# Experts by place: each token only through its two experts, from lines sorted in memory

## The reference

```
x = x + attn_a(layernorm(x))   # per batch a 64x64 rotation polynomial, a codebook row, RMS norm
x = x + experts(layernorm(x))
x = x + attn_b(layernorm(x))   # 16 heads of 8, softmax over 1024 tokens, output projection
x = x + experts(layernorm(x))  # the same weights again

experts(h):  logits = h @ router.T            # 8 experts
             top 2 of the logits, softmax over the two
             y_e = relu(h @ w1[e])**2 @ w2[e] # w1[e] 128x256, w2[e] 256x128
             out = sum over the two chosen e of weight * y_e
```

## Time and profile before

| | |
|---|---|
| median of three runs | 1290.02 us |
| profiled execution, its time | 1291.25 us |
| its span, first to last instruction | 1289.5 us |
| mean granted TensorE clock | 0.960 |
| PE, DVE, ACT, POOL busy | 93%, 76%, 75%, 22% |
| DMA queue of SP | 6014 packets, 9.45 MB, 2.1% of 16 engines |

### The profile page before, as it was taken

The page is one execution under the profiler, slowest core; times in us unless marked ns, Lnnn a source line. Parts: engine busy times, 40 slices in busy tenths (PEclk is TensorE's granted clock), DMA queues, the critical chain, the costliest instruction groups (busy, mean ns, idle before and its releaser), DMA issues.

```text
span 1289.5 us, 25719 instructions
## 1 busy us (share of the span) xinstructions
PE 1197.6 (93%) x10019; PEld 742.1 (58%) x10019; DVE 976.4 (76%) x2357; ACT 960.9 (75%) x1826; POOL 285.5 (22%) x326
## 2 busy tenths in 40 slices
PE   1779999998899999999999999999999999999998
PEld 1369999987434434444444444444444348999998
DVE  7575677766888898989898888988889814565654
ACT  1037777765158998888898888988888996777775
POOL 2032000003423333332332333332322100000000
PEclk9679999999569999999999999999999999999999
DMA  5100000000000000000000000000000000000000
GB/s 193 36 1 1 1 1 1 2 1 1 1 1 1 2 1 2 2 1 2 2 2 1 2 2 1 2 1 2 1 2 1 1 2 1 9 17 9 10 9 17
DMA packets 6134, 11.08 MB, mean 9 GB/s; under 512 B 1907, under 2 KB 3574, under 8 KB 5878
## 3 DMA queue, kind: packets, MB, share of 16 engines
q1 hardware_dynamic: 6014, 9.45, 2.1%
HBM read 7.28 MB, written 2.10 MB: 7 GB/s over the span
## 4 chain that ended last, share of the span: by engine, by line
PE 78%; DVE 13%; ACT 6%; issue 3%; DMA 0%; SPq 0%; ACTq 0%; DVEq 0%
PE acc L1280 17%; PE six L1115 17%; PE six L1251 10%; DVE mxp L947 8%; PE six L1103 6%; PE six L1105 5%; PE six L1104 5%; PE misc L1251 5%; ACT PB L645 3%; PE six L1264 2%; PE six L1217 1%; ACT SC L634 1%; PE six L1127 1%; PE six L1212 1%; PE misc L1103 1%
## 5 line engine op out<-in xcount | busy, mean ns | idle before, releaser
L947 DVE TENSOR_REDUCE mxp<-six 128x2 f32<-128x1024 f32 x512 | 598.8, 1219 | 75.4 <-PE six L1264 73.4
L645 ACT ACTIVATE PB<-six 128x512 f32<-128x512 f32 x681 | 384.9, 599 | 60.7 <-PE six L1251 36.9
L1280 PE MATMUL acc<-PB,Vg 128*32 128x256 f32 x4096 | 328.0, 392 | 16.3 <-ACT SC L634 16.3
L1264 PE MATMUL six<-K,Q 32*128 32x512 f32 x1024 | 264.1, 519 | 14.4 <-DVE mxp L947 9.7
L1251 PE MATMUL six<-Q,K 32*128 32x512 f32 x681 | 272.5, 498 | 0.1
L1115 PEld LDWEIGHTS six<-w2s,PB 128*128 128x128 f32 x2048 | 248.2, 192 | 11.3 <-ACT PB L547 0.7
L1115 PE MATMUL six<-w2s,PB 128*128 128x128 f32 x2048 | 249.3, 275 | 0.1
L850 DVE SCALAR_TENSOR_TENSOR x<-six,wexp,x 128x128 f32<-128x128 f32 x512 | 144.2, 345 | 134.9 <-PE six L1115 134.2
L541 ACT ACTIVATE PB<-six 128x512 f32<-128x512 f32 x256 | 151.2, 599 | 114.8 <-PE six L1105 104.4
L645 ACT ACTIVATE PB<-misc 128x512 f32<-128x512 f32 x343 | 205.4, 599 | 23.2 <-PE six L1251 17.1
L1251 PEld LDWEIGHTS six<-Q,K 32*128 32x128 f32 x681 | 107.9, 183 | 142.7 <-ACT PB L645 73.4
(11 more groups left out here) (225 smaller groups left out, 1094.7 us busy)
## 6 DMA issues: line engine op xcount, KB each, us to landing
x<-in_x SPq DMA_DIRECT2D x4, 512.0 KB, 5.1
SC<-in_w_om SPq DMA_DIRECT2D x1, 2048.0 KB, 14.6
out<-x SPq DMA_DIRECT2D x8, 256.0 KB, 2.0
VH<-in_w SPq DMA_DIRECT2D x1, 1024.0 KB, 9.2
Vg<-in_wqs SPq DMA_DIRECT2D x1, 256.0 KB, 8.0
Vg<-in_wks SPq DMA_DIRECT2D x1, 256.0 KB, 7.4
cst<-in_cst SPq DMA_DIRECT2D x1, 81.5 KB, 3.4
nwb<-in_nw SPq DMA_DIRECT2D x1, 64.0 KB
```

Of the source, the lines that this page charges most:

```text
L645: act.activation(PB[:, s % 3, j, :], scores, ACT.Exp).then_inc(G_("act_taken"), 1)
L947: dve.reduce_max(dst, taken_slot("max", s, i).rearrange("p (a n) -> p a n", a=2), AX.X).then_inc(G_("max_taken"), 1)
L1264: ins = pe.matmul(slot[:, c * BLK:(c + 1) * BLK], Q[rows, G % NG, t * P:(t + 1) * P], K[rows, G % NG, th * BLK:(th + 1) * BLK], start=True ...
L1280: ins = pe.matmul(acc[RB * j:RB * (j + 1), n], Vg[:, G % 2, t, j, :], PB[:, s % 3, j, n], start=(t == 0 and half == 0), stop=(t == TPB - 1 ...
```

## The change

The dense expert layer goes, in both layers. Each batch of 1024 tokens has 2048 (token, expert) pairs. They get a place in a list sorted by expert, in which each expert's part is rounded up to whole tiles of 128 lines; `RT` = 23 tiles hold every case. Per batch, for layer f:

- DVE normalises the batch (`rows`), PE transposes and runs the router in fp32 (`turn_rows`, `batch_router`), DVE takes the top two (`batch_top_two`), PE counts by triangular and all-one matmuls how many pairs stand before each (`batch_rank`, 16 matmuls), DVE works out the place of each pair and the expert of each tile (`batch_places`): `dest`, `te` (for SP) and `tw` (for PE).
- GpSimd sends each of the batch's 8 tiles of tokens twice to its places in a DRAM buffer `xs` (`send`, 16 indirect DMAs of 128 rows of 512 bytes). SP has filled the buffer with zeros at the start (`empty_lines`).
- SP loads the sorted lines in six groups of up to four tiles (`load_lines`), and, for each tile, the w1 of its expert from DRAM by a register (`load_weights`, 23 DMAs of 128 KB, three groups ahead). The registers are read from `te`, up to four at a time. w1 is no longer kept or split.
- PE reads up to four registers from `tw`, transposes the lines (`turn_lines`), makes the hidden values by fp32 matmuls of 128x128 (`lines_hidden`, a pair of tiles at a time), DVE takes relu (`relu_pair`), ACT squares (`square_pair`), PE makes the results two pairs later with w2 addressed by register (`lines_result`), ACT copies out the transposed lines and the results (`lines_out`, `result_out`), SP stores the results to a DRAM buffer `yd` (`keep_lines`).
- GpSimd fetches the two result rows of each token (`fetch`, 16 indirect DMAs), DVE adds them with their weights (`add_results`).

Where things stand: in layer 0 batches 0 and 1 are routed before the loop, 2 and 3 beside batches 0 and 1. Results of batch 0 are fetched and added during batch 3, those of batches 1 to 3 during attention (`late_results`, and GpSimd's fetches in groups -1 to 3), where the statistics for attention now stand too (`late_stats`). `attention_begin` follows the loop. In layer 1 batches 0 to 2 are routed in the last attention group (`routed_late`), batch 3 beside batch 0; `attention_end` runs as one piece before the loop; results of batches 1 to 3 are added after it. `RMS_GROUPS` has four groups. GpSimd builds the triangle `tri` at the start. The diff, cut to its core:

```diff
-RMS_GROUPS = ((0, 2), (2, 2), (4, 4))
+RMS_GROUPS = ((0, 2), (2, 2), (4, 2), (6, 2))
...
+LN_BLOCKS = (NBLK, 0, NBLK)
+SEND = 2 * TPB
+RT = (2 * L + E * (P - 1)) // P
+TG = 4
+RGROUPS = -(-RT // TG)
+PAIRS = -(-RT // 2)
...
+            def send(f, b):
+                n = sparse_index(f, b)
+                pl.wait_ge(G_("dest_ready"), n + 1)
+                if f == 0:
+                    pl.wait_ge(G_(f"emptied{b}"), 16)
+                for i in range(TPB):
+                    for k in range(2):
+                        pl.indirect_dma_start(xs[b], bass.IndirectOffsetOnAxis(ap=dest[:, b, k, i:i + 1], axis=0),
+                                              hbs[:, b, i, :], None).then_inc(G_(f"sent{b}"), 16)
...
+            def fetch(f, b, i):
+                for k in range(2):
+                    pl.indirect_dma_start(lines_back[b][:, k, i, :], None, yd[b],
+                                          bass.IndirectOffsetOnAxis(ap=dest[:, b, k, i:i + 1], axis=0)
+                                          ).then_inc(G_(f"back{b}{i // TPK}"), 16)
...
+            def load_lines(f, b):
+                n = sparse_index(f, b)
+                sp.wait_ge(G_(f"sent{b}"), 16 * SEND * (f + 1))
+                if n >= 2:
+                    sp.wait_ge(G_("lines_turned"), RGROUPS * (n - 1))
+                for g in range(RGROUPS):
+                    if n:
+                        sp.wait_ge(G_(f"line{g}"), 16 * (min(TG, RT - TG * g) + 1) * n)
+                    if f and b == 0 and g == 4:
+                        sp.wait_ge(G_("act_filled"), len(AR))
+                    t = slice(TG * g, min(RT, TG * (g + 1)))
+                    sp.dma_start(lines_in[b][:, t, :], xs[b].rearrange("(r p) d -> p r d", p=P)[:, t, :]
+                                 ).then_inc(G_(f"line{g}"), 16)
...
+            def load_weights(f, b, g):
+                n = RGROUPS * sparse_index(f, b) + g
+                sp.wait_ge(G_("te_ready"), sparse_index(f, b) + 1)
+                if n >= 3:
+                    sp.wait_ge(G_("hidp_done"), pair_count(n - 3))
+                for i, e in enumerate(expert_values(SP, te, b, g, E - 1)):
+                    sp.dma_start(w1t[:, n % 3, i * HID:(i + 1) * HID],
+                                 a["w1"][ds(e, 1)].rearrange("o d h -> (o d) h")).then_inc(G_(f"line{g}"), 16)
...
+                for m in range(RGROUPS * B):
+                    if m % RGROUPS == RGROUPS - 3 and m // RGROUPS + 1 < B:
+                        load_lines(f, m // RGROUPS + 1)
+                    if m + 3 < RGROUPS * B:
+                        load_weights(f, *divmod(m + 3, RGROUPS))
+                    if m:
+                        keep_lines(f, *divmod(m - 1, RGROUPS))
...
-            low_part(3, 0)
-            for n in range(1, NBLK):
-                low_part(3, n)
+            for b in range(3):
+                send(1, b)
+            fetch_batch(1, 0)
+            send(1, 3)
+            for b in range(1, B):
+                fetch_batch(1, b)
...
+            def batch_rank(f, b):
+                pe.wait_ge(G_("both_ready"), sparse_index(f, b) + 1)
+                if f == 0 and b == 0:
+                    pe.wait_ge(G_("tri_ready"), 1)
+                rank, all_lines = route_bank(f, b)[:, 128:128 + TPB * E], route_bank(f, b)[:, 192:192 + E]
+                pe.matmul(rank, tri[:], both[:], start=True, stop=False, skip_group_check=True)
+                for d in range(1, TPB):
+                    pe.matmul(rank[:, d * E:], ones[:], both[:, 0:(TPB - d) * E], start=False, stop=(d == TPB - 1),
+                              skip_group_check=True)
+                for i in range(TPB):
+                    ins = pe.matmul(all_lines, ones[:], both[:, i * E:(i + 1) * E], start=(i == 0), stop=(i == TPB - 1))
+                ins.then_inc(G_("rank_done"), 1)
...
+                link(dve.tensor_scalar(tilesi[:], route_bank(f, b)[:, 192:192 + E], float(P - 1), None, ALU.add))
+                link(dve.tensor_scalar(tilesi[:], tilesi[:], 7, None, ALU.arith_shift_right))
+                link(dve.tensor_copy(tilesf[:], tilesi[:]))
+                link(dve.tensor_tensor(upsum[:], tilesf[:].rearrange("p (o e) -> p o e", o=1).broadcast_to([P, E, E]),
+                                       upto[:], ALU.mult))
+                link(dve.reduce_sum(ends[:], upsum[:], AX.X))
+                link(dve.tensor_tensor(firstr[:], ends[:], tilesf[:], ALU.subtract))
+                link(dve.tensor_scalar(firstr[:], firstr[:], float(P), -1.0, ALU.mult, ALU.add))
+                link(dve.tensor_tensor(place[:], rank, firstr[:].rearrange("p (o e) -> p o e", o=1)
+                                       .broadcast_to([P, TPB, E]), ALU.add))
...
+            def turn_lines(f, b, g):
+                n = RGROUPS * sparse_index(f, b) + g
+                pe.wait_ge(G_("tw_ready"), sparse_index(f, b) + 1)
+                pe.wait_ge(G_(f"line{g}"), line_count(f, b, g))
+                if f and b == 0 and g == 1:
+                    pe.wait_ge(G_("acc_stored"), 8 * B)
+                if n >= 2:
+                    pe.wait_ge(G_("lines_stored"), n - 1)
+                for i, at in enumerate(expert_values(PE, tw, b, g, CH * D * (E - 1))):
+                    r = TG * g + i
+                    expert_at[b, r] = at
+                    ins = pe.transpose(line_bank(n)[:, i * P:(i + 1) * P], lines_in[b][:, r, :], ident)
...
+                        ins = pe.matmul(big[:, n % 2, at:at + P], tile_weights(group, r % TG, c), lines,
+                                        start=True, stop=True)
...
+                        ins = pe.matmul(big[:, 2 + group % 2, r % TG * D:(r % TG + 1) * D], sqs[:, n % 3, at:at + P],
+                                        w2f[:, ds(expert_at[b, r] + c * D, D)],
...
+                turn_lines(f, 0, 0)
+                for s in range(PAIRS * B):
+                    b, q = divmod(s, PAIRS)
+                    if q % 2 == 0 and s + 2 < PAIRS * B:
+                        turn_lines(f, *divmod(s // 2 + 1, RGROUPS))
+                    lines_hidden(f, b, q)
+                    if s >= 2:
+                        lines_result(f, *divmod(s - 2, PAIRS))
+                    route = routed_beside(f, b)
+                    if route and q in (5, 6):
+                        turn_rows(f, route, q - 5)
+                    elif route and q == 7:
+                        batch_router(f, route)
+                    elif route and q == 9:
+                        batch_rank(f, route)
...
+            def add_results(f, b, u):
+                dve.wait_ge(G_(f"back{b}{u}"), 16 * TPB * (f + 1))
+                for k in range(2):
+                    for i in range(TPK * u, TPK * (u + 1)):
+                        xt = x[:, b * L + i * D:b * L + (i + 1) * D]
+                        ins = dve.scalar_tensor_tensor(out=xt, in0=lines_back[b][:, k, i, :],
+                                                       scalar=pw[:, b, k, i:i + 1], in1=xt, op0=ALU.mult, op1=ALU.add)
+                    if k == 0:
+                        link(ins)
+                ins.then_inc(G_("mixed"), 1)
...
+            late_stats = {(0, 1): 2, (0, 9): 3, (2, 9): 4, (3, 9): 5, (4, 9): 6, (5, 9): 7}
+            late_results = {(-1, 14): (1, 0), (-1, 15): (1, 1), (1, 4): (2, 0), (2, 4): (2, 1), (3, 4): (3, 0),
+                            (4, 4): (3, 1)}
```

More of the change, by code:

```diff
@@ L310, in bank_a2, with line_bank, route_bank, rows_bank @@
             return six[:, n, :] if n < 6 else acc[:] if n == 6 else six[:, 3, :]
+        def line_bank(n):
+            return acc[:] if n % 2 else s1[:, 0, :]
+        def route_bank(f, b):
+            return six[:, 0, :] if f == 0 and b == 0 else s1[:, 1, :]
+        def rows_bank(f, b):
+            return six[:, 3, :] if f and b < 3 else misc[:]
+        def pair_count(n):
+            return PAIRS * (n // RGROUPS) + min(PAIRS, 2 * (n % RGROUPS) + 2)
+        def line_count(f, b, g):
+            return 16 * (min(TG, RT - TG * g) + 1) * (sparse_index(f, b) + 1)
+        def wait_kept(engine, f, b):
+            for k in range(3):
+                engine.wait_ge(G_(f"kept{k}"), 16 * RGROUPS // 3 * (sparse_index(f, b) + 1))
+        def tile_weights(n, i, c):
+            return w1t[:, n % 3, i * HID + c * P:i * HID + (c + 1) * P]
+        def first_bank(task):
+            return misc[:] if task % 2 else acc[:]
+        def routed_beside(f, b):
+            return (b + 2 if b < 2 else None) if f == 0 else 3 if b == 0 else None
+        def expert_values(engine, values, b, g, top):
+            _, experts = nc.values_load_multi_w_load_instructions(
+                values[0:1, b, TG * g:min(RT, TG * (g + 1))], engines=[engine], min_val=0, max_val=top,
+                skip_runtime_bounds_check_because="DVE bounds each of them when it writes them")
+            return experts
         @block.sync
@@ L450, in _ @@
             low_part(2, 0)
[L451 removed]
             low_part(2, 1)
[L453 removed]
+            for t in range(4):
```

(24 more changed lines are left out.)

656 lines of the change are left out of this document (413 added, 243 removed).

## The result

The changed kernel takes 1470.98 us (median, 1469.26 to 1472.79), the kernel before 1289.88 in the same comparison: ratio 1.1404, 95% interval 1.1384 to 1.1424, slower. The forecast was 1182 us. Times are medians of all executions of a kernel, ratios leave out the executions in a slower state, so that the two can differ a little (E6, E16).

What follows compares the result with a forecast made beforehand. It took TensorE to bound the expert layers (98% busy), with PE 96%, DVE and ACT 88% busy in attention. 1289.5 - 63 (layer 0) + 12 + 17 - 74 (layer 1) = 1181.5 us of span; predicted 1182, range 1125 to 1275.

Steps and rivals of the forecast that it cites:

- The indirect DMA: GpSimd's sends and fetches: 1.2 us each, bounds 0.46 and 2.03; a batch's 16 sends take 19.2 us.
- batch 3's chain: Layer 1: batch 0's results stored, 16 fetches, 16 sends, load; 74 us, wanted at 77, so hidden.
- TensorE per batch, 26.8 us: Expert layers' batch pace: matmuls 20.5 us, transposes 2.4, register reads 4; 26.8 us against 54.
- First expert matmul at 131.5: Layer 0's start: routing, sends, landing and line load put the first expert matmul at 131.5 us, 38 later.
- fits with nothing to spare; from 1.4 us an issue on, TensorE waits: Layer 0, batch 2's sends: start after destinations (157), land before batch 2 (about 179); 16 x 1.2 + 4.5 us.
- SP costs 16 us a batch: SP's queue in the expert layers: 35 issues at 0.46 us, 16 us a batch, six register reads on top.
- My rival of transfers and SP: Expert layers: transfers or SP set the pace, 36 us a batch, adding 74 us, total 1256; chance 0.20.
- Attention +12: Attention: added DVE results and statistics cost 5.5 us in the prelude and 6.5 elsewhere, 12 us longer.
- The last group +17: Attention's last group: added transposes, router and rank matmuls 19 us, 5.5 hidden, waits 3.5; 17 us longer.
- My rival of a low clock: Expert layers: TensorE falls to half clock, a batch takes 50 us, total 1368; chance 0.04.
- The tail of 29 us: Layer 1's end: copy, store, sixteen fetches, landing, results and last store after TensorE's last matmul, 29.4 us.
- GpSimd as the bound: Indirect DMAs in GpSimd's one queue are the bound; gain gone at about 2.4 us each, 1345 at 3.0; chance 0.12.

Runs made afterwards that it cites:

- E6: E1 with w1 kept in SBUF, each tile taking a fixed expert's, so the 184 weight loads go and results are other ones: 1333.86 us, 1.0310.
- E16: E13 with layer 0's line loads for batches 1 to 3 issued by GpSimd behind its own sends, not by SP: 1321.69 us, 1.0215.
- E4: The kernel before, plus four bursts of 16 back-to-back indirect fetches in the dense layer 1, which nothing waits for: 1350.66 us, 1.0472.
- E1: The changed kernel, with GpSimd waiting after every fourth indirect DMA of a send or whole-batch fetch until those landed: 1361.38 us, ratio 1.054.
- E15: The changed kernel with the changes of E2, E6 and E7, and attention's results and statistics in small parts, all at once: 1193.06 us, 0.9255.
- E13: E10 with the wait after every fourth indirect DMA in place of every sixth: 1309.62 us, 1.0170.
- E14: E10 with the wait after every second indirect DMA: 1386.19 us, 1.0761.
- E10: The changed kernel with waits after every sixth indirect DMA, E7's places, results and statistics in parts, layer 1's batch 3 sent before batch 0's fetch: 1345.43 us, 1.0429.
- E7: E1 with places found by two 64-column matmuls a batch in place of sixteen narrow ones, plus small DVE steps: 1350.84 us, 1.0461.
- E5: The kernel before, plus 56 indirect fetches in the dense layer 1, in fours with a wait for landing between: 1289.57 us, 0.9994.
- E11: The kernel before, plus four bursts of 12 indirect fetches in the dense layer 1, each followed by a GpSimd fill, no landing wait: 1289.88 us, 0.9994.
- E12: E4 with rows of 64 bytes in place of 512: 1350.74 us, 1.0457.
- E2: The changed kernel with sends and fetches as plain GpSimd DMAs of the same size, fixed places, lines not sorted: 1293.91 us, 1.0012.

## Why the prediction was wrong

The step that failed is the one headed *The indirect DMA*. Its size was right: 0.96 us, one per 1.26, where I took 1.2. What failed is that I costed it on GpSimd's queue alone, and put its effect on the work beside it at nothing without a reason: "The first three batches' sends run on GpSimd beside it", batch 3's chain "hidden up to 1.3 us an issue". Sends and fetches in runs of 16 stop the engines that they were to hide behind: 15 us a run where nothing else differs (E4). The pauses are 110 of the 289 us by E1, mostly in layer 0, in the last group and in layer 1. The other terms that were too small follow below. No run gives each of them a share of the rest; E15 shows that together they are most of it, since with all of them away the kernel is 278 us faster, some 24 of which I put down to the shorter GpSimd steps.

Point by point:

- *TensorE per batch, 26.8 us*: a little high where nothing stops it. Two neighbouring pairs of tiles begin 2.22 us apart in PE's timeline of the changed kernel, with transposes of the routing between them, and 11.5 pairs are 25.5 us; E15's last two batches, without routing, took 23 and 24. That is the 22.9 of matmuls and transposes alone: the 4 us for register reads don't show.

```profile
165.38 1.06 PE L1481 MATMUL six<-VH,w1t 128*128 128x128 f32 x8
...
167.60 1.06 PE L1481 MATMUL six<-VH,w1t 128*128 128x128 f32 x8
```

- *First expert matmul at 131.5*: 136.2; destinations at 101, not 106. The second batch's routing, which goes ahead of it, lies beside the first run of sends.
- *Sends: "fits with nothing to spare; from 1.4 us an issue on, TensorE waits"*: right, and it came true in E13 and E14, where the waits make it 1.5 and 2.0 us an issue.
- *SP costs 16 us a batch*: too little. With waits and lines in the same queue the weights came late; without them the kernel is 27 us faster (E6). My rival of transfers and SP was right in kind; its 74 us were too much.
- *Attention +12*: it was +66; +54 in E1, +27 in E13. The prelude came out as forecast (+5.5 in its second half). The rest lies in half groups 2 to 13, counted from the prelude's first as 0, ten of which got new DVE work; the last 18 are as before to 0.1 us. (Nine blocks at 0.65 us are 5.9 us, not the 6.5 of the sum.) I had read 0.65 us for a block of statistics from one half group. A lump of eight sums took 4.06 us in one step, 508 ns each in place of the 345 of the earlier trace rows (DVE's timeline below), and PE's clock fell in these half groups: it is 0.85 in half groups 2 to 13, where the kernel before has 0.98. They take 320 us in E1, 270 in the kernel before, and 293 in E13, with the lumps cut up. E10 and E16, with the same code there, have 304 and 313 at a lower clock, so part of E13's gain may be a kinder clock. The indirect fetches have no part in it, since E15, without them, has 292. What the other 23 us are was not tried.

```profile
520.22 4.06 DVE L1158 SCALAR_TENSOR_TENSOR x<-hbs,pw,x 128x128 f32<-128x128 f32 x8
```

- *The last group +17*, +25 with the output projection that I put in layer 1: +83 in the changed kernel, up to layer 1's first expert matmul; +61 in E1, +43 in E13. I priced the narrow matmuls at full clock. The stage's mean clock is 0.58, and the router's sixteen records in it take 3.58 us (below) where layer 0 has them in 1.85 at full clock. My rival of a low clock was about the layers and had 0.04: it argued that PE at half clock would be "fully busy" again, and so would not stay there. In the last group of E1 PE is busy 94% and the mean clock is 0.60 all the same; in the changed kernel's layers it is 0.75 and 0.74, where the stopped issue leaves gaps (E1 has 0.87 in layer 0). That the narrow matmuls bring the clock down, as E7's shorter stage suggests, is argued, not shown.

```profile
1164.07 3.58 PE L1436 MATMUL six<-rwf,tr 128*128 128x8 f32 x16
```

- *The tail of 29 us*: 33, from 1438.1 to the end, with sixteen fetches in 19.9.

The rival that came out on the right side, GpSimd as the bound, has another mechanism: it wanted more than 2.4 us per indirect DMA, and in the changed kernel there is one per 1.26. Only in E13 and E14, where waits stretch the queue, does its mechanism hold in layer 1. The mean of the sends is 0.96 us busy, also beside DVE's work, and the longest of all 256 indirect DMAs is 1.17. The Trainium skill's "SBUF — State Buffer", section A bandwidth-pool intuition that's wrong, would have had them near 3.1 us there; this trace has no such row; whether any DVE step here is of the kind that the page measured these runs don't show. The harm goes the other way: the DMAs stop DVE, and no row shows DVE stopping them. The other rule that I cited, the Trainium skill's "DMA: Bandwidth & Descriptors", section Bandwidth (0.95 us for 64 KB from GpSimd), lies by the 0.96 of the trace, but the two count different times, the page the DMA engines' and the trace GpSimd's own, so the agreement shows nothing.

The largest fault is one of method: for an operation without a row I bounded its own duration from both sides, but not its effect on the others, and the two rivals that would have made the kernel slower held 0.16 together.

## What to carry to other kernels

Indirect DMAs of GpSimd are not work beside other work: in fours with a wait for landing, or 1.8 us apart, they cost the others nothing (E5, E11), in runs of eight and more they stop all of them. The waits stretch GpSimd's own queue to 1.5 to 2.1 us per DMA, so count them all, or that queue is the next bound. Price an instruction that the trace has never shown by what else could stop, not by its own time alone, and run it once beside the old kernel first (E4 would have told it). Lumps of DVE work beside a nearly full TensorE cost more than their time (18 us for 11 in E1's four half groups, 6 once cut up): cut them up. Many fp32 matmuls of a few columns may be dear in the same way; two of 64 columns in place of sixteen made the stage 8 to 18 us shorter.

## What the runs showed of the hardware that was not expected

- From about the ninth of a run of indirect DMAs on (11 us in, at one per 1.26 us) PE, DVE, ACT and SP all but stop issuing, also instructions that wait for nothing, until some 3 us after the last (3.5 in E4, 2.8 in the changed kernel at 1183.6); sixteen cost 15 us (E4). The bytes don't matter (64 bytes a row or 512, E12), and both sends and fetches do it. SP's register steps are hit sooner: in the changed kernel 3.5 us into a run (141.0), and now and then in E1's fours.
- Plain DMAs of GpSimd with the same rows take 0.54 us each and have no such effect in runs of 16 (E2).
- At one indirect DMA per 1.76 us, with a fill on GpSimd between two of them, there is no effect at all, with no wait for landing (E11).
